# Residual addition, norm and routing behind the first self attention put into one block

## What is computed

```python
x = x + _L0_attn_ref(_layernorm(x, axis=-1), ...)
x = x + _L0_ffn_ref(_layernorm(x, axis=-1), L0_ffn_w_router, L0_ffn_w1, L0_ffn_w2, L0_ffn_bias)

def _layernorm(x, axis=-1, eps=1e-05):
    m = jnp.mean(x, axis=axis, keepdims=True)
    v = jnp.var(x, axis=axis, keepdims=True)
    return (x - m) / jnp.sqrt(v + eps)

def _L0_ffn_ref(x, w_router, w1, w2, bias):
    ...
    scores = jax.nn.softmax(xf @ w_router, axis=-1)
    expert_weights, top_experts = jax.lax.top_k(scores, TOP_K)      # 2 of 8
    ...                                # the first 256 tokens of each expert, in order
    h = jax.nn.gelu(jnp.einsum('ech,ehf->ecf', xb, w1))
    y = jnp.einsum('ecf,efh->ech', h, w2).reshape(E * capacity, hs)
    ...                                # back to the tokens, times their weights
    return out.reshape(sl, bs, hs) + bias
```

## Time and profile before

| | |
|---|---|
| Time, median of 3 runs | 1368.52 us (1367.79 to 1369.06) |
| Time of the profiled execution | 1370.81 us |
| Its span | 1369.0 us |
| PE / weight loads / DVE busy | 1233.9 (90%) / 1036.5 (76%) / 972.0 us (71%) |
| ACT / POOL busy | 784.7 (57%) / 634.9 us (46%) |
| Mean granted clock of PE | 0.935 |

### The profile page before, as it was taken

How to read it: one execution, slowest core, us unless ns; L and a number is a source line. 1 busy time by engine, 2 the same in 40 slices (tenths; PEclk the granted TensorE clock), 3 DMA queues, 4 the chain that set the end, 5 groups by cost and what they waited for, 6 DMA issues and landing times. The chain is left out here.

```text
span 1369.0 us, 35013 instructions
## 1 busy us (share of the span) xinstructions
PE 1233.9 (90%) x12294; PEld 1036.5 (76%) x12294; DVE 972.0 (71%) x1995; ACT 784.7 (57%) x1435; POOL 634.9 (46%) x580
## 2 busy tenths in 40 slices
PE   5999999999999689539998999999999999777778
PEld 4788888888888458429985788888888888546455
DVE  5777777777777576456526877777777777578896
ACT  3677777777776211115444677777777776224221
POOL 3666656656664214032332656566656654325000
PEclk9999999999999885559999999999999999887999
DMA  7786776776765120434537776776776765100000
GB/s 223 208 212 177 184 203 175 185 202 178 190 166 139 45 55 2 152 132 152 198 131 223 198 202 177 191 195 176 179 207 175 189 168 135 37 0 3 1 8 24
DMA packets 106725, 198.33 MB, mean 145 GB/s; under 512 B 43661, under 2 KB 63790, under 8 KB 106640
## 3 DMA queue, kind: packets, MB, share of 16 engines
q1 hardware_dynamic: 105104, 193.32, 52.8%
q0 software_dynamic: 1536, 3.88, 0.8%
HBM read 88.26 MB, written 10.62 MB: 72 GB/s over the span
## 5 line engine op out<-in xcount | busy, mean ns | idle before, releaser
L913 POOL TENSOR_SCALAR cross_prob<-cross_prob,cross_inverse 128x1024 f32<-128x1024 f32 x256 | 287.7, 1124 | 327.5 <-DVE cross_inverse L647 327.5
L844 ACT ACTIVATE cross_prob<-cross_negated,cross_negmax 128x1024 f32<-128x1024 f32 x256 | 295.0, 1152 | 135.7 <-DVE cross_negmax L639 135.4
L639 DVE CUSTOM_DVE_ANT_0 cross_negated<-cross_scores,cross_bias 128x1024 f32<-128x1024 f32 x256 | 313.6, 1225 | 25.7 <-PE cross_scores L513 8.1
L526 PEld LDWEIGHTS cross_turn<-ident,cross_prob 128*128 128x128 f32 x2048 | 237.9, 140 | 47.3 <-POOL cross_prob L913 9.7
L526 PE MATMUL cross_turn<-ident,cross_prob 128*128 128x128 f32 x2048 | 268.0, 273 | 6.3 <-POOL cross_prob L913 4.6
L853 ACT COPY cross_probT<-cross_turn 128x512 f32<-128x512 f32 x256 | 149.4, 584 | 63.6 <-PE cross_turn L526 62.7
L655 DVE COPY cross_probT<-cross_turn 128x512 f32<-128x512 f32 x256 | 175.5, 686 | 0.0
L513 PE MATMUL cross_scores<-cross_keys,cross_qbd 96*128 96x512 f32 x512 | 169.5, 412 | 2.8 <-POOL cross_qbd L905 2.8
L893 POOL TENSOR_TENSOR cross_ctx_lo<-cross_raw,cross_ctx_hi 128x512 fp32r<-128x512 f32 x120 | 154.7, 1291 | 14.1 <-DVE cross_probT L715 8.3
L456 PE MATMUL cross_out<-cross_wv_hi,cross_ctx_lo 128*128 128x256 f32 x488 | 147.4, 302 | 0.0
L458 PE MATMUL cross_out<-cross_wv_hi,cross_ctx_hi 128*128 128x256 f32 x488 | 137.3, 281 | 0.0
(11 more groups left out here) (283 smaller groups left out, 2120.3 us busy)
## 6 DMA issues: line engine op xcount, KB each, us to landing
cross_keys<-cross_key_hi SPq DMA_DIRECT2D x512, 128.0 KB, 2.4
cross_raw<-in_ctxT SPq DMA_DIRECT2D x32, 1024.0 KB, 5.6
cross_keys<-cross_key_lo SPq DMA_DIRECT2D x256, 128.0 KB, 2.4
cross_bias<-bias_rows SPq DMA_DIRECT2D x32, 512.0 KB, 3.7
up_sb<-in_moe_w SPq DMA_DIRECT2D x8, 1024.0 KB, 9.3
down_sb<-in_moe_w SPq DMA_DIRECT2D x8, 1024.0 KB, 5.7
cross_stacked_q<-q_rows SPq DMA_DIRECT2D x90, 64.0 KB, 2.0
q_rows<-cross_negated SPq DMA_DIRECT2D x8, 256.0 KB, 2.3
```

Of the source, the lines that this page charges most:

```text
L526: last = pe.transpose(ps_t[part][:, k * P:(k + 1) * P], prob[n % 2][:, kt * P:(kt + 1) * P], ident)
L639: dve.tensor_tensor_reduce(negated[n % 2], ps_s[n % 2][:, :], bias_sb[par][:, :], -1.0, 3.0e38, ALU.add, ALU.min, negmax[:, n % 2:n % 2 + ...
L844: act.activation(prob[n % 2][:, :], negated[n % 2], ACT.Exp, bias=negmax[:, n % 2:n % 2 + 1], scale=-1.0, accum_out=total[:, n % 2:n % 2 + ...
L913: pool.tensor_scalar(prob[n % 2][:, :], prob[n % 2][:, :], inverse[:, n % 2:n % 2 + 1], 1.0, ALU.mult, ALU.mult).then_inc(prob_ready, 1)
```

## The change

The three blocks become one, `route_block`, which takes `oT` and `x` as well. `normalize_block` stays for the other stages. Within the one block:

- DVE takes the moments as before, but adds eps (`variance`) for the first four tiles as soon as their moments are there, and for the other four at the end. POOL takes the power for each half (128x4, twice). DVE normalizes all tiles behind its last addition.
- PE transposes and multiplies by turns, a pair of tiles at a time, the transposes one pair ahead of the products.
- SP issues the eight tables first, then `gate_up`, then `xn` in two halves as they are ready, then the experts' weights, and `down` last. PE waits for the tables (`tables_loaded`) behind the first pair's transposes; the wait for the weights (`loaded`) is at the end of the block.

The new code of the block, with what it replaces cut out:

```diff
-def add_turned_block(nc, tag, aT, ident, x, moments, loads):
...
+def route_block(nc, tag, aT, x, ident, xn, xnT, w_router, rank_from, before, all_ones, places, columns, ids, weight, gather_at,
+                scatter_at, stored_rows, tables, weights):
...
         @block.sync
         def _(sp):
-            sp.dma_start(stored_rows.rearrange("(i p) d -> p i d", p=P), xn[:, :, :]).then_inc(rows_stored, 16)
-            for out, in_ in loads:
+            for out, in_ in tables:
+                sp.dma_start(out, in_).then_inc(tables_loaded, 16)
+            sp.dma_start(*weights[0]).then_inc(loaded, 16)
+            for half in range(2):
+                sp.wait_ge(normed, NT // 2 * (half + 1))
+                sp.dma_start(stored_rows.rearrange("(h i p) d -> h p i d", h=2, p=P)[half], xn[:, NT // 2 * half:NT // 2 * (half + 1), :]
+                             ).then_inc(rows_stored, 16)
+            for out, in_ in weights[1:]:
                 sp.dma_start(out, in_).then_inc(loaded, 16)
-            sp.wait_ge(rows_stored, 16)
-            sp.wait_ge(loaded, 16 * len(loads))
+            sp.wait_ge(rows_stored, 32)
+            sp.wait_ge(loaded, 16 * len(weights))
+
+        @block.gpsimd
+        def _(pool):
+            clear_semaphores(nc, pool)
+            for half in range(2):
+                at = slice(NT // 2 * half, NT // 2 * (half + 1))
+                pool.wait_ge(stat_step, half + 2)
+                pool.tensor_tensor(rstd[:, at], variance[:, at], power[:, at], ALU.pow).then_inc(rooted, 1)
 
         @block.tensor
         def _(pe):
+            def turn_tokens(j):
+                if j >= 2:
+                    pe.wait_ge(copied, j - 1)
+                for i in (2 * j, 2 * j + 1):
+                    pe.wait_ge(normed, i + 1)
+                    for g in range(G):
+                        at = (g * 2 + i % 2) * P
+                        last = pe.transpose(ps_t[j % 2][:, at:at + P], xn[:, i, g * P:(g + 1) * P], ident)
+                last.then_inc(turned, 1)
+
+            def logits(j):
+                pe.wait_ge(copied, j + 1)
+                for i in (2 * j, 2 * j + 1):
+                    for k in range(G):
+                        last = pe.matmul(ps_l[:, i, :], xnT[:, k, i * P:(i + 1) * P], w_router[:, k, :],
+                                         start=(k == 0), stop=(k == G - 1))
+                if j == NT // 2 - 1:
+                    last.then_inc(logits_ready, 1)
+
             for i in range(NT):
-                for k in range(G):
...
+                if i >= 2:
+                    pe.wait_ge(added, i - 1)
+                for g in range(G):
+                    last = pe.transpose(ps_b[i % 2][:, g * P:(g + 1) * P], aT[:, g, i * P:(i + 1) * P], ident)
+                last.then_inc(attended, 1)
+            turn_tokens(0)
+            pe.wait_ge(tables_loaded, 16 * len(tables))
+            for j in range(NT // 2):
+                if j + 1 < NT // 2:
+                    turn_tokens(j + 1)
+                logits(j)
...
+            for j in range(NT // 2):
+                act.wait_ge(turned, j + 1)
+                act.copy(xnT[:, :, j * 2 * P:(j + 1) * 2 * P], ps_t[j % 2][:, :].rearrange("p (g t) -> p g t", g=G)
+                         ).then_inc(copied, 1)
...
+            def see(i):
+                dve.wait_ge(added, i + 1)
+                dve.bn_stats(stats[:, i, :], x[:, i, :]).then_inc(seen, 1)
+
+            def aggregate(i):
+                dve.wait_ge(seen, 2 * i + 1)
+                dve.bn_aggr(moments[:, i, :], stats[:, i, :]).then_inc(seen, 1)
+                if i % (NT // 2) == NT // 2 - 1:
+                    at = slice(i + 1 - NT // 2, i + 1)
+                    dve.wait_ge(seen, 2 * i + 2)
+                    dve.tensor_scalar(variance[:, at], moments[:, at, 1], EPS, None, ALU.add).then_inc(stat_step, 1)
+
+            dve.memset(power[:, :], -0.5).then_inc(stat_step, 1)
+            for i in range(NT):
+                dve.wait_ge(attended, i + 1)
+                dve.tensor_tensor(x[:, i, :], x[:, i, :], ps_b[i % 2][:, :], ALU.add).then_inc(added, 1)
+                if i:
+                    see(i - 1)
+                    aggregate(i - 1)
+            see(NT - 1)
+            aggregate(NT - 1)
+            for i in range(NT):
+                if i % (NT // 2) == 0:
+                    dve.wait_ge(rooted, i // (NT // 2) + 1)
+                dve.tensor_scalar(xn[:, i, :], x[:, i, :], moments[:, i, 0:1], rstd[:, i:i + 1],
+                                  ALU.subtract, ALU.mult).then_inc(normed, 1)
+            dve.wait_ge(tables_loaded, 16 * len(tables))
             dve.wait_ge(logits_ready, 1)
```

More of the change, by code:

```diff
@@ L1440, in route_block @@
         counted, ranks_ready, marked, table_ready = sem("counted"), sem("ranks_ready"), sem("marked"), sem("table_ready")
-        loaded, rows_stored = sem("loaded"), sem("rows_stored")
+        loaded, tables_loaded, rows_stored = sem("loaded"), sem("tables_loaded"), sem("rows_stored")
+        stats, moments, rstd = sb("stats", [P, NT, 6]), sb("moments", [P, NT, 2]), sb("rstd", [P, NT])
+        variance, power = sb("variance", [P, NT]), sb("power", [P, NT])
+        ps_b = [ctx.enter_context(nc.psum_tensor(f"{tag}_b{i}", [P, D], F32)) for i in range(2)]
+        ps_t = [ctx.enter_context(nc.psum_tensor(f"{tag}_turn{i}", [P, 2 * D], F32)) for i in range(2)]
+        attended, added, seen, stat_step, rooted = sem("attended"), sem("added"), sem("seen"), sem("stat_step"), sem("rooted")
+        normed, turned, copied = sem("normed"), sem("turned"), sem("copied")
         block = ctx.enter_context(nc.Block())
@@ L1446, in _ @@
         def _(sp):
-            sp.dma_start(stored_rows.rearrange("(i p) d -> p i d", p=P), xn[:, :, :]).then_inc(rows_stored, 16)
-            for out, in_ in loads:
-                sp.dma_start(out, in_).then_inc(loaded, 16)
-            sp.wait_ge(rows_stored, 16)
-            sp.wait_ge(loaded, 16 * len(loads))
+            for out, in_ in tables:
[5 more added lines that the diff above has]
+                             ).then_inc(rows_stored, 16)
@@ L1453, in _ @@
         @block.tensor
         def _(pe):
-            for i in range(NT):
-                for k in range(G):
-                    last = pe.matmul(ps_l[:, i, :], xnT[:, k, i * P:(i + 1) * P], w_router[:, k, :],
-                                     start=(k == 0), stop=(k == G - 1))
-            last.then_inc(logits_ready, 1)
+            def turn_tokens(j):
[7 more added lines that the diff above has]
+                last.then_inc(turned, 1)
@@ L2183, in attend, with experts @@
                 scope.pop()
-        def experts(finish_last, first, result):
+        def experts(first, result):
             with ExitStack() as own:
@@ L2214, in perceiver @@
             result = [own.enter_context(nc.sbuf_tensor(f"result{i}", [P, CAPACITY // P, D], F32)) for i in range(2)]
-            experts(lambda loads: add_turned_block(nc, "self0_add", oT, eye, x, moments, loads), first, result)
+            experts(first, result)
             cross(1, first, taken={"results": results, "loaded": taken_loaded, "weight": weight})
```

52 lines of the change are left out of this document (7 added, 45 removed).

## The result

The changed kernel takes **1366.38 us** (median of 12 runs, 1362.90 to 1368.69), the kernel before, measured beside it, 1368.82 us (12 runs): a ratio of **0.9972, with a 95% interval of 0.9959 to 0.9985**, so 3.8 us faster (2.1 to 5.6). The two medians lie 2.44 us apart (0.9982), which the interval holds too. I had forecast 1363.6 us, which is 4.9 us less than a median of 1368.52, and a range of 1361.0 to 1366.0. The ratio applied to that median gives 1364.7 us, inside the range; the median of 1366.38 as it stands lies 0.4 us above it. Two single executions further down, of the changed kernel's third measurement (2448 us) and of the kernel without the second power (2449 us), are left out of their ratios. The profiled execution took 1366.63 us.

A forecast was written before the change was run, and what follows sets the result against it. Between 563 and 580 us a single file of engines, each waiting for the one before, was taken as the bound; 4.4 + 0.93 - 0.3 - 0.1 = 4.9 us off the 1368.52 median gave 1363.6 us, range 1361.0 to 1366.0.

The forecast's parts named there:

- Normalizing starts earlier: Between VectorE's last aggregate and first normalizing instruction: start at 563.40 instead of 567.81, 4.4 us earlier.
- The two `variance` instructions: On VectorE's path, one in the middle and one at the end: together 0 to 0.5 us, taken as 0.35.
- PE's part: Router's transposes and products: 0.93 us gap goes, four more changes cost 0.3 (0 to 0.8), on a fixed 10.72 us.
- POOL beside VectorE: POOL's power running beside VectorE's normalizing could slow VectorE by 0 to 0.8 us, taken as 0.1.
- Tables: Small tables, ahead of big weights on SP's queue, land before PE asks: no cost, 1.7 us if the last took 7.4.
- Big transfers: Rows and experts' weights plus `down` land at 585.5 where the block would end at 594.9: hidden, 9 us to spare.
- Clock of PE in the stretch: PE without a gap over 0.3 us from first `moe_xn` transposition to last product, at a clock of 0.50.
- The rival of a full clock: Rival that PE gets its full clock; chance 0.07.
- The experts' clock: Slower rival: experts' products meet a clock that stays low, each microsecond costing half a one, time 1371.3 us; chance 0.05.
- From logits to the cast: From first logits on VectorE to first cast of the experts: chain left as it is, distance staying 19.9 us.
- The sum: Whole gain: 4.4 + 0.93 - 0.3 - 0.1 = 4.9 us, taken from the median of 1368.52 to 1363.6 us.
- My own sign of being wrong: Wrong if logits-to-cast distance grew, PE stood for the tables, or stretches behind, the experts above all, took another time.

The follow-up runs named there:

- third measurement: The changed kernel run a third time without a change, against the kernel before; ratio 0.9970 (0.9955 to 0.9985).
- the kernel without the second power: Changed kernel with POOL's power for the first half only, whose values also scale the second half's tiles; ratio to the kernel before 0.9973.
- one power: Changed kernel with a single 128x8 power behind the last aggregate instead of two halves; ratio to the kernel before 0.9966.
- pairs: Changed kernel with power, normalizing and transposes by pairs of tiles, the first two pairs normalized between additions; ratios to the kernel before 0.9954 and 0.9953.
- the order of the loads alone: Kernel before with only the two big weights moved to the end of the routing block's loads, three blocks kept; ratio to the kernel before 0.9963.
- warm kernel: Changed kernel with extra PE products nobody reads, behind each added tile's transposes and before the first `moe_xn` is transposed; ratio to the kernel before 0.9936.

## Why the prediction was right

**Normalizing starts earlier: right, to 0.03 us.** Forecast 4.4 us, measured 12.54 - 8.11 = 4.43. Its parts, the barrier with the late table (2.84, of which 2.27 table and 0.57 barrier) and the hidden power, are both shown by a run. The two `variance` instructions, forecast at 0.35 us, cost 0.33: the last aggregate ends 0.21 us later in the stretch than before (7.99 and 7.78 us behind its start), and `moe_xn` starts 0.12 us behind it. The first power lay free as said.

**PE's part: right in direction, mis-sized.** I had 0.93 for the gap, less 0.3 for four more changes between transposes and products, less 0.1 for POOL, so 0.53 between the start of the transposes and the logits. Measured was 11.69 - 10.39 = 1.30. The step that failed is the sum 10.72 + 0.3: to take 3.76 and 6.96 us as fixed and add a tail for each change. Each of these lengths already held the tail of its last instruction, which the barrier had PE wait out; without it each first product starts before the last transposition ahead of it has ended (568.84 against 569.02), and the changes cost nothing: the whole is 10.28 us. With all transposes first it is 10.38, the products taking 6.83 us there for a reason that the rows don't show. The end of PE's work fell below my lower bound for it, 10.72, which I had taken for a floor.

**POOL beside VectorE: right that it is small, wrong about who pays.** VectorE's normalizing instructions kept their length, 408 ns; POOL's second power took 1.25 us where the first took 1.01, so it ended at 568.01, when the fifth normalizing instruction was due at 567.93. The fifth `moe_xn` started some 0.15 us later for it, whence 2.83 instead of 2.67 us. PE had tiles in hand, so none of my 0.1 us arrived on the path. The power began behind the first normalizing instruction (566.76 against 566.59) and is the one that grew; but it grew by 0.24 us in all while several normalizing instructions of 408 ns ran, so the trace doesn't show it held up for even one whole instruction, nor why it is the one that pays.

**Tables: right.** They landed in 1.8 to 3.2 us with nothing big ahead of them, against 5.3 to 7.4. Had they stood behind the big weights, the price was 0.66 us, and I had 1.7.

**Big transfers: right.** 9.8 us to spare, forecast over 9. **Clock of PE in the stretch: right**, 0.50 throughout and 10.28 us of 10.28 busy. The rival of a full clock (0.07) didn't come.

**The experts' clock: the rival came in a small size.** It was to cost time if the experts' products stayed at the low clock for longer, and in the changed kernel's trace they did, where before the clock stood at 1.00 from 616.0 and, by the products' distance, from 614.9:

```profile
608.55:612.40 3.85, 3.85 (x18) 3.85 (x19) 3.71 (x5) 1.29 (x3) 3.85 (x6) 0.50 0.00 1
613.00:614.00 1.00, 1.00 (x6) 1.00 (x6) 0.99 (x1) 0.18 (x1) 0.17 (x1) 0.50 0.00 0
614.00:616.00 2.00, 2.00 (x16) 2.00 (x15) 0.96 (x1) 0.90 (x3) 0.00 (x0) 0.82 0.00 0
```

From their first product (608.55 here, 610.92 before) until products follow at the short distance it is 6.2, 4.0 and 5.7 us in the three traces of the changed kernel, against 4.0, 3.4 and 3.5 before. From the cast to the end of the experts' last product it is 119.3, 118.4 and 119.0 us, against 118.3, 117.9 and 118.4: 0.7 us more in the mean, for 1.7 us more at the low clock. In the other kernels of one block the low clock lasted 3.4 to 5.5 us, so chance is not excluded. Behind the experts PE's clock fell once more, in the second cross attention, in all three traces of the changed kernel and in one of three of the kernel before. In eight of the fourteen traces of the table it fell, to 0.50 for some 3 to 7 us (in the changed kernel's, 0.50 from 735.5 to 737.5), and there the way from the cast to the last `cross_rstd` took 146.5 to 146.9 us; in the six others, where it stood at 1.00 up to that row, it took 143.6 to 144.3. Whether the change makes this fall more frequent isn't shown.

**From logits to the cast: 20.05 instead of 19.93 us.** Forecast was no change. 0.13 us of it is the idle time of 0.16 us between `route_top` and `route_logit`. It is there in the changed kernel and also without the second power, and gone with one power (19.91) and with pairs (19.97), with the same two instructions there; I have no cause for it.

**The sum**: 4.43 + 1.30 - 0.12 is the 5.62 us but for rounding; forecast 4.9. In total time three measurements of the changed kernel gave 0.9972, 0.9963 and 0.9970, mean 0.9968 or 4.3 us; 5.62 us would be a ratio of 0.9959, which lies in the intervals of two of them and at the edge of the third. By the ratio the median of 1368.52 becomes 1364.7, inside the range. So the number was hit by a local gain 0.7 us larger and a total some 1.3 us smaller than that gain, and that the two errors offset each other is luck. Where the remainder lies stays open, since stages that the edit doesn't touch scatter by more: between the means of the three traces of either kernel, the stretch starts 2.3 us later after the change, is 5.6 shorter, the way from the cast to the last `cross_rstd` is 1.9 longer, and the rest 1.5 shorter. My own sign of being wrong, that the stretches behind take another time, can't be told from chance with three traces each. That total time can't rank such variants is seen in the table: the order of the loads alone, 2.28 us in the stretch, measured 0.9963 as well, and all transposes first, 0.10 us longer in the stretch than the changed kernel, 0.9945.

## What to carry to other kernels

When a barrier is idle time's releaser, look first at which transfer kept it shut: putting eight small loads ahead of two large ones gave two fifths of what a rewrite of three blocks gave (2.28 of 5.62 us). Busy times of two groups of instructions with a barrier between them aren't fixed terms, since each contains a tail that overlapped here once the barrier was gone (10.28 us from the first to the last, where 3.76 and 6.96 make 10.72). And measure a change of this size between two anchors around it, where the same program repeats within 0.04 us, since the total scatters by some us (1362.90 to 1368.69 in the changed kernel's 12 runs).

## What was not expected of the hardware

- **A busy PE did not get the high clock here.** The changed kernel's PE was busy for 10.28 us of 10.28 and was granted 0.50 all through, and in the warm kernel it was granted 1.00 at 564.20, but 0.50 from 566.30 on, at 2.00 us busy of 2.00 and 5.40 of 5.40. The experts' products of the kernel before, as busy, were granted 0.50 from 610.90 to 614.80 and 1.00 from 616.00 on the earlier trace rows; what sets them apart from the router's isn't shown.
- **The power on POOL has a fixed part of about 0.4 us, by my estimate** from three lengths, 0.70 us for 128x2, 1.01 for 128x4 and 1.64 for 128x8. So two halves cost more POOL time than one whole (2.02 us against 1.64), and paid here because the first was hidden.
- **A barrier that no transfer holds up** left VectorE idle for 0.57 us between an aggregate and the next block's first instruction.
- **Which of VectorE and POOL pays differs**: in the earlier trace rows a normalizing instruction took 1.34 us, where it takes 408 ns otherwise, beside POOL's operation on 128x512; beside the power of 128x4 VectorE's instructions kept their length and POOL's took 0.24 us more.
